# VectorE takes the low half of the second norm, TensorE turns the rows of the first two items, and the written order of every engine is replaced

## The reference, cut to what matters

```
h = layernorm(x) * (1 + ca) + sa                     # x: 8 batches x 1024 rows x 128
for i in range(6):                                   # six layers
    xn = layernorm(x, ln1)
    q, k, v = xn @ wq, xn @ wk, xn @ wv              # 8 heads of 16
    attn = softmax(q, -1) @ (softmax(k, rows)^T @ v)
    x = attn @ wo + bo + x
    xn = layernorm(x, ln2)                           # the second norm
    x = leaky_relu(xn @ w1) @ w2 + x                 # 128 -> 512 -> 128
x = x + ga * (the above)
h = layernorm(x) * (1 + cb) + sb
x = x + gb * fp4_ffn(h)                              # gate and up to 352, silu, down to 128
```

## Time and profile before

| what | value |
|---|---|
| median of 3 runs | 1203.79 us (1203.06 to 1204.75) |
| the profiled execution | 1201.45 us |
| its span in the trace | 1199.4 us |
| busy: PE, PEld, DVE, ACT, POOL | 93%, 71%, 90%, 86%, 91% |
| granted TensorE clock, mean | 0.969 |

### The profile page before, as it was taken

The page is one execution under the profiler, slowest core; times in us unless marked ns, Lnnn a source line. Parts: engine busy times, 40 slices in busy tenths (PEclk is TensorE's granted clock), DMA queues, the critical chain, the costliest instruction groups (busy, mean ns, idle before and its releaser), DMA issues.

```text
span 1199.4 us, 29698 instructions
## 1 busy us (share of the span) xinstructions
PE 1111.5 (93%) x9494; PEld 848.2 (71%) x9494; DVE 1081.2 (90%) x2892; ACT 1029.9 (86%) x1770; POOL 1089.8 (91%) x920
## 2 busy tenths in 40 slices
PE   7556899999999999999999999999999988999996
PEld 5443777777777777777777777777787755565664
DVE  7999889999999999999999999999987589999972
ACT  5757899999999999999999999999999895767662
POOL 4888999999999999999999999999999988999762
PEclk8577999999999999999999999999999999999998
DMA  8354667768777776676777876867777320110000
GB/s 307 112 170 123 203 197 224 198 202 214 187 216 196 197 221 193 191 212 197 216 195 192 216 199 197 218 193 207 203 195 220 107 71 18 36 37 36 18 19 36
DMA packets 218903, 197.54 MB, mean 165 GB/s; under 512 B 113952, under 2 KB 196224, under 8 KB 218752
## 3 DMA queue, kind: packets, MB, share of 16 engines
q1 hardware_dynamic: 218752, 195.65, 57.3%
HBM read 90.73 MB, written 79.69 MB: 142 GB/s over the span
## 4 chain that ended last, share of the span: by engine, by line
PE 49%; POOL 23%; issue 14%; DVE 9%; ACT 2%; DMA 1%; SPq 1%; DVEq 0%; POOLq 0%; ACTq 0%
POOL hidden L1685 10%; PE pair L548 4%; POOL rows_split L1677 4%; PE pair_mlp L528 4%; PE pair L519 4%; PE pair_mlp L507 4%; PE ring_pair L560 3%; PE mlp L644 3%; PE ring_pair L562 3%; PE ring_pair L561 3%; PE pair_mlp L618 3%; POOL arena L1691 2%; POOL arena L1658 2%; PE pair_mlp L629 2%; PE mlp L577 2%
## 5 line engine op out<-in xcount | busy, mean ns | idle before, releaser
L1685 POOL TENSOR_TENSOR hidden<-hidden 128x2048 f16<-128x2048 f32 x92 | 376.2, 4089 | 0.0
L793 ACT ACTIVATE hidden<-ring_pair,hidden_bias 128x512 f32<-128x512 f32 x384 | 245.7, 686 | 31.6 <-PE ring_pair L562 31.5
L802 ACT ACTIVATE hidden<-hidden 128x2048 f16<-128x2048 f32 x96 | 183.4, 1911 | 17.3 <-PE mlp L577 14.7
L1004 DVE BATCH_NORM_STATS2 bn<-x_all 128x6 f32<-128x128 f32 x896 | 184.2, 277 | 4.1 <-DMA x_all<-in_L_attn_x 0.9
L1611 POOL TENSOR_TENSOR rstd<-ve,minus_half 128x8 f32<-128x8 f32 x104 | 170.5, 1639 | 0.0
L763 ACT ACTIVATE arena<-x_all,nmr,rstd 128x128 f32<-128x128 f32 x384 | 157.9, 495 | 0.8 <-POOL nmr L1672 0.8
L560 PE MATMUL ring_pair<-arena,halves 128*128 128x512 f16 x384 | 146.0, 380 | 8.8 <-ACT hidden L793 3.4
L562 PE MATMUL ring_pair<-arena,halves 128*128 128x512 f16 x384 | 146.4, 381 | 0.0
L561 PE MATMUL ring_pair<-arena,halves 128*128 128x512 f16 x384 | 146.2, 381 | 0.0
L575 PE MATMUL mlp<-halves,hidden 128*128 128x128 f16 x768 | 135.9, 219 | 1.4 <-issue 1.4
L577 PE MATMUL pair_mlp<-halves,hidden 128*128 128x128 f16 x768 | 136.0, 219 | 0.0
(11 more groups left out here) (190 smaller groups left out, 3092.4 us busy)
## 6 DMA issues: line engine op xcount, KB each, us to landing
n_away<-all_blocks SPq DMA_DIRECT2D x48, 512.0 KB, 3.0
norm_raw<-n_away SPq DMA_DIRECT2D x192, 128.0 KB, 3.3
k_away<-all_blocks SPq DMA_DIRECT2D x48, 512.0 KB, 2.8
q_away<-all_blocks SPq DMA_DIRECT2D x48, 512.0 KB, 3.3
arena<-k_away SPq DMA_DIRECT2D x192, 128.0 KB, 3.4
arena<-q_away SPq DMA_DIRECT2D x192, 128.0 KB, 3.6
x_all<-in_L_attn_x SPq DMA_DIRECT2D x8, 512.0 KB, 5.4
x_in<-in_L_attn_x SPq DMA_DIRECT2D x8, 512.0 KB, 4.2
```

Of the source, the lines that this page charges most:

```text
L793: act.activation(hidden_t[:, c * W + h * HALF:c * W + (h + 1) * HALF], ring[n % 2], ACT.Prelu, bias=hidden_bias[:, b:b + 1], scale=HIDDEN_ ...
L802: act.activation(half_rows(hidden_hi, h), half_rows(hidden_t, h), ACT.Copy).then_inc(hidden_hi_ready, 1)
L1004: last = nc.vector.bn_stats(bn[:, 6 * t:6 * t + 6], src(t))
L1685: pool.tensor_tensor(half_rows(hidden_lo, h), half_rows(hidden_t, h), half_rows(hidden_hi, h), ALU.subtract).then_inc(hidden_lo_ready, 1)
```

## The change: what it does

1. `second_norm_low` is taken from POOL and given to DVE: the same operation on the same tiles.
2. `POOL_TILES` goes from 3 to 4: POOL makes four tiles of the first norm, ACT four.
3. For the first item (`FIRST_N = 1`) the norm, and for the first two (`FIRST = 2`) the k and q tiles, are no longer transposed by DVE and sent through memory. PE turns them with eight transposes each into a PSUM pair (`turn_first_n`, `turn_first_k`, `turn_first_q`), and ACT copies them out (`first_norm_t`, `copy_k`, `copy_q`).
4. The lists `items(v)` of all engines are written anew, in other orders and with other items in a turn. DVE now adds the attention of item v−3 in turn v and takes the maximum of k of item v−1, where it was v−4 and v−2; ACT, POOL and DVE run one or two turns less in all.

```diff
-    POOL_TILES = 3
+    POOL_TILES = 4
+    FIRST_N, FIRST = 1, 2
...
+        first_k = [k_exp, k_blocks]
...
             def send_n(i):
+                if i < FIRST_N:
+                    return
                 sp.wait_ge(n_blocks_ready, i + 1)
...
+            def turn_first_n(i):
+
+                pe.wait_ge(norm1_ready, i + 1)
+                pe.wait_ge(norm1_rest_ready, i + 1)
+                for t in range(T):
+                    last = nc.tensor.transpose(tile(S0, t), tile(norm1[i % NB], t), identity[:, :])
+                last.then_inc(n_blocks_ready, 1)
+
+            def turn_first_k(i):
+
+                pe.wait_ge(bo_added, 1)
+                pe.wait_ge(k_exp_t_ready, i + 1)
+                after(pe, q_prob_t_ready, 16 * QB * i)
+                for t in range(T):
+                    last = nc.tensor.transpose(tile(ring_pair, t), tile(k_exp_t, t), identity[:, :])
+                last.then_inc(k_blocks_ready, 1)
...
+            def copy_k(i):
+
+                act.wait_ge(k_blocks_ready, i + 1)
+                after(act, z_done, i - 1)
+                act.activation(first_k[i % 2], ring_pair[:, :], ACT.Copy).then_inc(k_exp_ready, 16 * QB)
...
             def block_k(i):
+                if i < FIRST:
+                    return
                 dve.wait_ge(k_exp_t_ready, i + 1)
-                after(dve, k_blocks_away, 16 * i)
+                after(dve, z_done, FIRST)
+                after(dve, k_blocks_away, 16 * (i - FIRST))
...
+            def second_norm_low(i):
+                dve.wait_ge(rows_hi_ready, i + 1)
+                after(dve, norm2_lo_ready, 16 * i)
+                nc.vector.tensor_tensor(rows_lo, norm2, rows_hi, ALU.subtract).then_inc(rows_lo_ready, 1)
...
-                if on(v - 4): add_attention(v - 4)
...
+                if on(v - 4): second_norm_low(v - 4)
...
+                if on(v - 3): add_attention(v - 3)
...
-            def second_norm_low(i):
-                pool.wait_ge(rows_hi_ready, i + 1)
-                after(pool, norm2_lo_ready, 16 * i)
-                pool.tensor_tensor(rows_lo, norm2, rows_hi, ALU.subtract).then_inc(rows_lo_ready, 1)
```

More of the change, by code:

```diff
@@ L407, in items @@
                 if 46 <= v < 46 + 2: load_back(v - 46)
-            for v in range(ITEMS + 3):
+            for v in range(ITEMS + 4):
                 items(v)
@@ L498, in hidden_bias_cols, with keep_warm, turn_first_q @@
                 last.then_inc(w1_turned, 1)
+            mlp0_bank = mlp[0]
+            filler = identity[:, :].bitcast(F16)
+            def keep_warm(bank, count, semaphore=None, value=0):
+                if semaphore is not None:
+                    pe.wait_ge(semaphore, value)
+                for n in range(count):
+                    nc.tensor.matmul(bank[:, 0:2 * P], filler[:, 0:P], filler, start=True, stop=True)
+            def turn_first_n(i):
[11 more added lines that the diff above has]
+                last.then_inc(k_blocks_ready, 1)
+            def turn_first_q(i):
+                pe.wait_ge(q_prob_ready, i + 1)
+                pe.wait_ge(k_exp_ready, 16 * QB * (i + 1))
+                for t in range(T):
+                    last = nc.tensor.transpose(tile(ring_pair, t), tile(q_prob, t), identity[:, :])
+                last.then_inc(q_blocks_ready, 1)
             def product_k(i):
@@ L527, in product_z @@
                 for t in range(T):
-                    last = nc.tensor.matmul(S1[:, 0:D], tile(norm1[i % NB], t), rows[:, t], start=(t == 0), stop=(t == T - 1))
+                    last = nc.tensor.matmul(S1[:, 0:D], tile(norm1[i % NB], t), tile(first_k[i % 2], t) if i < FIRST else rows[:, t],
+                                            start=(t == 0), stop=(t == T - 1))
                 last.then_inc(z_done, 1)
@@ L559, in first_mlp @@
                 after(pe, hidden_copied, PIECES * i + n - 1)
+                if i == 0 and n == 0:
+                    after(pe, q_prob_t_ready, 16 * QB * FIRST)
                 nc.tensor.matmul(ring[n % 2], hi, rows_hi, start=True, stop=False)
@@ L968, in items @@
[L968 to L975 removed]
+                if on(v): normalise1(v)
+                if v == 0: fold_weights()
+                if v == 2: copy_k(0)
+                if v == 2: front_hat(4)
@@ new lines, in items @@
+                if v == 53: x_lift(3)
+                if v == 53: hidden_inverse(1)
+                if v == 53: x_lower(3)
+                if v == 53: hidden_tile(2, 0)
+                if on(v - 4): moments2(v - 4)
+                if v == 51: x_scaled(0)
+                if v == 51: x_shifted(0)
+                if v == 51: x_moments(2)
+                if v == 51: x_max(0)
+                if v == 51: x_scale(0)
+                if v == 51: x_inverse(0)
+                if v == 51: hidden_low(46, 0)
@@ L1525, in items @@
[L1525 to L1535 removed]
+                if v == 1: front_stats(3)
```

391 lines of the change are left out of this document (200 added, 191 removed).

## The result

The changed kernel takes 1210.97 us in the median of 6 runs (1208.54 to 1216.47), the kernel before 1203.40 beside it (6 runs, 1201.47 to 1204.75). The ratio is 1.0072, with a 95% interval of 1.0056 to 1.0088. Forecast were 1192 us and a range of 1177 to 1212: the time lies inside the range, but the sign is wrong. The profiled execution has a span of 1208.7 us against 1199.4.

The account below looks back on a forecast made before the run. The prediction took PE's floor of 18.27 us a turn as the bound of the even stretch. Its terms −2 (even stretch), −4 (start) and −6 (far end) summed to −12, giving 1192 us, range 1177 to 1212.

Parts of the forecast that it names:

- PE's floor: Even stretch: PE's own work takes 18.27 us a turn, so at most 5.6 us could be won there.
- the term: Even stretch: mean turn taken as 18.35 against 18.41 us over 39 turns, −2 us, bounds −5.6 and +18.
- POOL is no longer a bound: Even stretch: POOL's work falls from 18.27 to 16.55 us a turn, and it waits some 1.7 us.
- DVE's 1.2 us for the subtraction: DVE's turn: the moved low-half subtraction of 1024 columns takes 1.2 us undisturbed.
- The lock: DVE and POOL exclude each other; subtraction goes first, DVE waits 0.1 us, POOL's 1.7 us slack covers a 1.2 stop.
- The start: First items: DVE spared transposes and add_attention reordered, −4 us, bounds 0 and −10.
- The step to item 2: Start: DVE needs about 24 us from add_attention of item 1 to that of item 2, instead of 28.8.
- The far end: Last item's way from added attention to last MLP half gets shorter, −6 us, bounds 0 and −12.
- the way from added attention to the last MLP half some 8 us shorter: Far end: by the new lists, the last item's 56.9 us shrink by up to 8.
- `second_mlp` following more closely: Far end: tile 0 in the turn of pieces 6 and 7, part of the some 8 us shorter way.
- "Slower": Whole kernel: slower by more than 2.4 us, chance 0.18.
- the power ahead of the subtraction: Lock rival: root1's power starts first each turn, DVE waits 1.64 us more, 1252 us (half the turns: 1220); chance 0.16.

Follow-up runs that it names:

- e3: Changed kernel with the low-half subtraction of items 0 to 45 back on POOL ahead of root1, three first-norm tiles on POOL, five on ACT, new orders kept: 1248.33 us.
- e4: Kernel before with only the low-half subtraction moved to DVE, between block_k and block_q, old orders and three POOL tiles: 1212.12 us.
- e6: Changed kernel with three tiles of the first norm on POOL and five on ACT: 1216.44 us.
- e9: Changed kernel with DVE's subtraction covering only 64 of 1024 columns from item 1 on, so products are not exact: 1207.35 us.
- e10: Changed kernel with DVE making the low half from one source tile times a constant (tensor_scalar), so another number: 1206.94 us.
- e5: Changed kernel without PE's turning: the rows of items 0 and 1 go through DVE and memory again, new orders kept: 1220.18 us.
- e1: Changed kernel with SP loading x back for the last stage a turn earlier, in turns 45 and 46: 1206.36 us.
- e2: e1 plus the third load of x moved ahead of the last item's two row transposes in SP's list: 1205.49 us.
- e11: e2 plus the root and offset of feed-forward unit 0 on POOL in turn 49 in place of 50: 1204.09 us.
- e13: e11 plus residual(3) placed behind root2 of item 47 in POOL's turn 50: 1206.34 us.
- e14: e13 plus SP issuing the next layer's four weight loads behind the second norm's row transposes of the next turn: 1207.74 us.
- e8: Changed kernel with PE turning only the norm of item 0; k and q tiles of items 0 and 1 go through memory: 1215.59 us.
- e12: Kernel before, old orders, with PE turning the norm of item 0 only: 1202.72 us.

## Why the prediction was wrong, step by step

- **PE's floor: the number right, the step wrong.** The even stretch's undisturbed turns last 18.27 us in both kernels. "No change here takes any work from PE's turn", so only 5.6 us could be won, holds. But I read it as if PE's floor covered the other engines' new waits. e3, e4 and e6 made turns of 19.39, 18.62 and 18.69 us with PE's work unchanged. Four engines that are busy 94% and more don't leave four slacks to spend: each wait can come back through the other lists. And I set the term below my own sum: DVE's turn came out at 18.45 in the middle, above PE's 18.27, and I took 18.35 without a reason. With 18.45 the term would have been +1.6 us and not −2.
- **POOL is no longer a bound: right and worth nothing** (e4). The idle POOL stands in front of `root1`, 0.8 us in the turn shown, not the 1 to 2 us I had named.
- **DVE's 1.2 us for the subtraction: right (1.21). The lock: the order right, its price wrong.** I let POOL's slack cover the stop. POOL's idle time lay ahead of `root1`, where it waits for the same `moments1`; the stop lies behind that, and no slack of POOL's is left there. It shows in ACT, which waits 11.9 us for it, and whose one tile less I had set at nothing though it is worth 4.0 to 5.5 us (e6). The even stretch came to +3.0 in place of −2. A short or quick subtraction takes back 2.1 to 2.3 (e9, e10).
- **The start: −4 forecast, −0.75 measured, by two terms that cancel.** The turning is worth 9.0 at item 3 (e5), not the few us that I gave it; the new orders without it cost 8.2, a term I didn't have. The step to item 2 was right (24.9 us against my 24), item 3 followed 18.27 later; "item 1 itself within 1 us of 97" was wrong, at 99.62 (97.8 to 99.6 in the runs with the same start).
- **The far end: −6 forecast, +7.1 measured (from +2.67 at item 44 to +9.78 at the last MLP half).** Three steps failed. First, I didn't go through the new places of the last stage's first steps: `residual(0)` 14.5 us earlier, its load 4.7. That is 4.6 us (e1). The third load's place I missed in the same way, 1.2 to 2.0 us (e2). Second, "the way from added attention to the last MLP half some 8 us shorter" set the even stretch's lag of 23.4 us against the new list's 20.5. But with no further items behind it the last item never had that lag: in the kernel before its first MLP piece ran at 971.96, 20.3 us behind its `add_attention` at 951.69. The new kernel's way with the loads mended is 20.8 to 21.3 (e2, e11, e13), so there was nothing to win. Third, the other 5 of the 8 us were to come from `second_mlp` following more closely, and I had no sum for them: from that piece to the last half both take 36 us (1007.88 − 971.96; 36.0 in e2), woven with the feed-forward units.
- **Less cover for transfers** was no rival of mine at all. The lag from `add_attention` to `first_mlp` is 20.9 us in the middle (20.5 to 22.0) in the even stretch in place of 23.6 (23.3 to 24.4), the row transposes stand in between, and PE's waits on transfers went from 0.9 to 4.6 us. Against before the even stretch lost 0.7 us with waits of 3.5 (e10), 0.9 with 2.9 (e9), 3.0 with 4.6 (after), 5.5 with 6.7 (e13), 5.7 with 5.9 (e14) and 14.5 with 14.7 (e8). Loss and waits go together, but not one to one, and which of them follows from the other isn't shown; e14 shows only that moving one group of transfers didn't lessen the sum by more than 0.8.
- **The rivals.** "Slower" had a chance of 0.18, nearly all of it for the power ahead of the subtraction; that didn't happen. The kernel became slower by causes that stood in no rival, and that 1210.97 still lies within 1177 to 1212 is luck.

Open is what holds the last 0.5 to 1.3 us between item 47's `add_attention` and the last MLP half (56.7 us in e2 and 57.5 in e11 against 56.2): neither the earlier root nor `root2`'s place took it away. In the old orders it was 56.2 in two executions and 56.8 in a third (e12), so part of it may be chance.

## What to carry to other kernels

Slack of an engine is a place in its list, not a sum: before a stop or a wait is booked as covered, look whether the idle time lies ahead of it or behind, and who waits for the next instruction. When orders are written anew, check every wait on a transfer against where its issue stands now; here one line in SP's list was worth 4.6 of 7.6 us. And read the last item's own way from its own rows; the lag of the even stretch isn't that of an item with nothing behind it.

## What the runs showed of the hardware

A DVE operation from one SBUF tile (`tensor_scalar`, 1024 columns in 0.68 us) stops a POOL instruction just as one from two tiles (1.21 us): POOL's lasted 0.72 and 1.25 us in place of 0.20. DVE's reductions beside POOL's power did not: the power took 1.63 us beside `sum_q`. The row transposes' issue on SP's queue took 1.24 us in most turns, and up to 2.75 us in some (changed kernel).
